# A gated cross-attention block on one core: where TensorE's transposes stand, and the order of an attention step

## The reference, cut to what matters

```python
x = x + tanh(g_xattn) * attention(layernorm(x), ctx, ctx)     # x: (2, 2048, 512), ctx: (2, 77, 512)
x = x + tanh(g_ffn)   * ffn(layernorm(x))

# attention, 16 heads of 32
q, k, v = q_in @ Wq.T, ctx @ Wk.T, ctx @ Wv.T
scores = einsum('bhqd,bhkd->bhqk', q, k) * SCALE
scores = where(row >= key, scores, -1e9)                       # 77 keys: masks the first rows only
out = einsum('bhqk,bhkd->bhqd', softmax(scores), v) @ Wo.T

# ffn, 512 -> 1536 -> 512, integer weights times 1/127
h = silu(x @ wg.T) * (x @ wu.T)
out = h @ wd.T
```

## Time and profile before

| | before |
|---|---|
| median of 3 runs | 873.64 us (873.36 to 874.93) |
| the profiled execution's own time | 874.07 us |
| its span, first to last instruction | 872.3 us |
| PE busy | 98% |
| DVE / ACT / POOL busy | 75% / 53% / 46% |
| mean granted clock of TensorE | 1.000 |

### The profile page before, as it was taken

The page is one execution under the profiler, slowest core; times in us unless marked ns, Lnnn a source line. Parts: engine busy times, 40 slices in busy tenths (PEclk is TensorE's granted clock), DMA queues, the critical chain, the costliest instruction groups (busy, mean ns, idle before and its releaser), DMA issues.

```text
span 872.3 us, 12869 instructions
## 1 busy us (share of the span) xinstructions
PE 855.0 (98%) x4087; PEld 707.9 (81%) x4087; DVE 652.8 (75%) x1081; ACT 460.5 (53%) x1130; POOL 402.3 (46%) x344
## 2 busy tenths in 40 slices
PE   8999999999999999999999999999999999999997
PEld 7678888888888887788888888888888888888876
DVE  5988877778786877679688478788487877587882
ACT  5687575666666757446056264165362364460550
POOL 4665555556564664437144444155253255251350
PEclk9999999999999999999999999999999999999999
DMA  9233847272728131567333256043265143243302
GB/s 334 73 109 118 276 152 248 84 240 93 233 97 277 68 113 51 198 235 265 115 123 133 96 190 249 12 165 121 79 248 182 47 164 113 96 166 116 97 31 98
DMA packets 60406, 128.73 MB, mean 148 GB/s; under 512 B 7616, under 2 KB 20416, under 8 KB 60352
## 3 DMA queue, kind: packets, MB, share of 16 engines
q1 hardware_dynamic: 58960, 125.95, 41.7%
q10 hardware_dynamic: 1392, 2.10, 0.7%
HBM read 99.93 MB, written 27.79 MB: 146 GB/s over the span
## 4 chain that ended last, share of the span: by engine, by line
PE 87%; DVE 6%; ACT 3%; issue 1%; DMA 1%; POOL 1%; ACTq 0%; DVEq 0%
PE psum L1814 34%; PE psum L1548 29%; PE psum L1864 18%; PE psum L1573 4%; DMA gates<-g_ffn 1%; PE psum L1657 1%; ACT e L791 1%; POOL hT L696 1%; DVE bn L1034 1%; DVE e L1076 1%; DVE K L1128 1%; DVE mx L1073 1%; DVE qT L1058 0%; DVE pT L1047 0%; DVE aT L1058 0%
## 5 line engine op out<-in xcount | busy, mean ns | idle before, releaser
L1814 PE MATMUL psum<-xv,ring 128*128 128x512 f32 x1344 | 308.2, 390 | 0.9 <-ACT a L964 0.7
L1814 PEld LDWEIGHTS psum<-xv,ring 128*128 128x128 f32 x1344 | 251.5, 188 | 55.1 <-ACT a L964 1.1
L696 POOL TENSOR_TENSOR hT<-th,hT 128x512 fp32r<-128x512 f32 x48 | 86.3, 1798 | 201.2 <-ACT hT L984 201.2
L1864 PE MATMUL psum<-w_d,hT 128*128 128x512 f32 x768 | 177.7, 391 | 1.3 <-POOL hT L696 0.8
L1864 PEld LDWEIGHTS psum<-w_d,hT 128*128 128x128 f32 x768 | 143.7, 188 | 32.6 <-POOL hT L696 2.0
L554 POOL TENSOR_TENSOR e<-e,rden 128x616 f32<-128x616 f32 x64 | 77.9, 1217 | 110.4 <-DVE rden L1110 73.8
L791 ACT ACTIVATE e<-psum,nmx,q_scale 128x77 f32<-128x77 f32 x256 | 102.6, 427 | 2.3 <-DVE nmx L1090 2.2
L952 ACT ACTIVATE a<-psum 128x512 f32<-128x512 f32 x48 | 28.7, 599 | 131.7 <-PE psum L1814 131.4
L1428 DVE SCALAR_TENSOR_TENSOR acc<-psum,gate_ffn,acc 128x512 f32<-128x512 f32 x64 | 47.7, 750 | 65.1 <-PE psum L1864 65.1
L1548 PE MATMUL psum<-wo,aT 128*128 128x512 f32 x384 | 95.2, 399 | 0.5 <-DVE aT L1058 0.5
L1548 PE MATMUL psum<-xT,wq 128*128 128x512 f32 x360 | 89.0, 398 | 0.4 <-DVE qT L1058 0.4
(11 more groups left out here) (110 smaller groups left out, 1204.6 us busy)
## 6 DMA issues: line engine op xcount, KB each, us to landing
ring<-w_var SPq DMA_DIRECT2D x48, 896.0 KB, 4.6
w_var<-stage SPq DMA_DIRECT2D x12, 896.0 KB, 4.6
x_ln<-x SPq DMA_DIRECT2D x32, 256.0 KB, 4.6
x_res<-x SPq DMA_DIRECT2D x32, 256.0 KB, 5.0
x_mid<-x_res SPq DMA_DIRECT2D x32, 256.0 KB, 2.0
x<-x_mid SPq DMA_DIRECT2D x16, 512.0 KB, 5.6
acc<-x_mid SPq DMA_DIRECT2D x16, 512.0 KB, 6.4
out<-acc SPq DMA_DIRECT2D x32, 256.0 KB, 2.0
```

Source lines behind the costliest of these rows:

```text
L696: nc.gpsimd.tensor_tensor(hT[:, 1, i % HH, j, :], h[:, :], hT[:, 0, i % HH, j, :].bitcast(f32), ALU.subtract).then_inc(h_lo, 1)
L1814: last = nc.tensor.matmul(psum[:, bank, :], stat, mov, start=start and j == 0, stop=j == len(terms) - 1, skip_group_check=not start)
L1864: last = nc.tensor.matmul(m_bank[t % 2][:, :], hT[:, a, m, t // TT, (t % TT) * P:(t % TT + 1) * P], w_d[:, HH * h + m, :], start=m == 0 an ...
```

## The change

Four things are drawn anew.

1. In blocks 1 to 6 the transposes of the probabilities no longer stand in runs. A helper `pieces` hands a product a function that issues one transpose behind each of its matmuls: `o(0, 0, 8, 0)` is the first projection with pieces 0 to 7 of tile 0, one behind each matmul from matmul 0; `o(1, 8, 10, 6)` the second with pieces 8 and 9 behind matmuls 6 and 7.
2. The order of a step: weighted product 0 stands between the two units of tile 0's scores; all transposes of tiles 2 and 3 go inside the query products, and query product 3 ends the step. VectorE's, ScalarE's and GpSimd's lists of a step are written anew to go with it (`last_step`, for block 7, keeps the order that it had).
3. At the end of attention, B22 and B21 go inside weighted products 2 and 3, and VectorE takes the four rests of the weighted products before T2 and T3 are formed.
4. At a pair's end, `p7` stands ahead of `p5` in the last slice, `p4` and `p3` follow at once, and all four groups go inside matmuls of `down`; `down` of tile 1 is cut behind slot 3 and not behind slot 5.

The number of matmuls and transposes stays what it was: 352 transposes (240 of probabilities, 112 of rows) now stand alone.

```diff
+            def pieces(n, t, first, end, at):
+                def after(j):
+                    if at <= j < at + end - first:
+                        turn_piece(n, t, first + j - at)
+                return after
 ...
-            def query(i, m):
+            def query(i, m, after=None):
                 m_wait(i)
                 product(m_bank[m % 2][:, :],
-                        [(wq[:, a, k, m * P:(m + 1) * P], xT[:, c, k, :]) for k in range(KD) for a, c in CROSS]
-                        ).then_inc(m_full, 1)
+                        [(wq[:, a, k, m * P:(m + 1) * P], xT[:, c, k, :]) for k in range(KD) for a, c in CROSS],
+                        after).then_inc(m_full, 1)
 ...
-            def step(n, b, b_before, masked, more):
+            def step(n, b, b_before, masked):
 ...
+                score_unit(n, 0, 0, b, masked, base - 2)
+                v(0)
+                score_unit(n, 0, 1, b, masked, base)
+                v(1)
+                v(2)
+                v(3)
+                scores(n, 1, b, False)
+                pe.wait_ge(m_free, base + 4)
+                pe.wait_ge(wo_split, 2)
+                o(0, 0, 8, 0)
+                o(1, 8, 10, 6)
+                scores(n, 2, b, False)
+                o(2, 0, 8, 0)
+                o(3, 8, 10, 6)
+                scores(n, 3, b, False)
+                pe.wait_ge(x_lo, 4 * n + 8)
+                q(0, 2, 0, 8, 0)
+                q(1, 2, 8, 10, 6)
+                q(2, 3, 0, 4, 6)
+                q(3, 3, 4, 10, 2)
 ...
-            for m in range(G):
-                values(M_LAST + m, m, B - 1, T_P2 - 2 + min(m, 2))
-                if m == 1:
-                    turn(0, B22)
-            turn(0, B21)
+            values(M_LAST, 0, B - 1, T_P2 - 2)
+            values(M_LAST + 1, 1, B - 1, T_P2 - 1)
+            values(M_LAST + 2, 2, B - 1, T_P2, turning(0, B22))
+            values(M_LAST + 3, 3, B - 1, T_P2, turning(0, B21))
 ...
-                    p5(i)
-                    p7(i)
+                    if m == MH - 1:
+                        p7(i)
+                        p5(i)
+                    else:
+                        p5(i)
+                        p7(i)
 ...
-                if more:
-                    turn(p + 1, B11)
-                    turn(p + 1, B12)
                 p4(last)
                 p3(last)
-                down(p, 1, 0, range(HH - 1))
-                down(p, 1, 1, range(HH - 1))
+                if more:
+                    first_k, second_k = turning(p + 1, B11), turning(p + 1, B12)
+                    down(p, 1, 0, range(HH - 1), lambda i: first_k(i) if i < KH * TT else second_k(i - KH * TT))
+                    down(p, 1, 1, range(HH // 2), lambda i: second_k(i + 2 * (HH - 1) - KH * TT))
+                else:
+                    down(p, 1, 0, range(HH - 1))
+                    down(p, 1, 1, range(HH // 2))
 ...
                 down(p, 1, 0, range(HH - 1, HH))
-                down(p, 1, 1, range(HH - 1, HH))
+                down(p, 1, 1, range(HH // 2, HH))
                 if more:
-                    turn(p + 1, B22)
-                    turn(p + 1, B21)
-                for t in range(2, PT):
+                    down(p, 1, 2, range(HH), turning(p + 1, B22))
+                    down(p, 1, 3, range(HH), turning(p + 1, B21))
+                for t in range(4 if more else 2, PT):
                     down(p, 1, t)
```

VectorE's list of a step (`slot(i)` is one tile of statistics: all eight in blocks 1 and 6, `slot` 1, 3, 4 and 5 in the others), up to the shift of tile 1, and the other lists in short:

```diff
+                slot_free(n, 0)
+                shift0(n, 0)
+                v_low(n, 0)
+                largest1(n, 0)
+                offset1(n, 0)
+                slot(0)
+                v_low(n, 1)
+                sum0(n, 0)
+                slot(1)
+                v_low(n, 2)
+                inverse0(n, 0)
+                denominator1(n, 0)
+                slot(2)
+                v_low(n, 3)
+                slot_free(n, 1)
+                shift(n, 1)
 ...
 (GpSimd)
-                probabilities(n, 0)
                 x_low_t(n + 1, (0, 1))
+                probabilities(n, 0)
+                build(n, 0)
                 probabilities(n, 1)
                 x_low_t(n + 1, (2, 3))
                 probabilities(n, 2)
-                if first:
-                    variance(n + 1)
-                build(n, 0, first)
+                build(n, 1)
 ...
 (VectorE, end of attention)
             for m in range(G):
                 m_low(H_LAST + m + 1, m, aT[:, 1, m, :], aT[:, 0, m, :])
-                if m == 1:
-                    form(0, T2)
-                if m == 2:
-                    form(0, T3)
+            form(0, T2)
+            form(0, T3)
+            residual(NB, 0)
             xv_low(0, B21, b21_at)
-            residual(NB, 0)
+            residual(NB, 1)
 ...
 (ScalarE, a pair's end)
-                if more:
-                    xv_copy(p + 1, B11, b11_at)
                 tanh2(last)
                 tanh1(last)
+                h_high(last, 0)
                 if more:
-                    b12_copy(p + 1)
-                h_high(last, 0)
+                    xv_copy(p + 1, B11, b11_at)
                 h_high(last, 1)
```

More of the change, by code:

```diff
@@ L386, in load_w, with residual @@
                     .then_inc(w_in[i % 3], 16)
-            def residual(n, first=False, ahead=False, keeps=((), ())):
+            def residual(n, first=False, ahead=False, keeps=((), (), ())):
                 for t in range(TT):
@@ L400, in residual @@
                     sp.dma_start(mid_f[n - 1, :, t, :], x_res[:, t, :]).then_inc(mid_out[t], 16)
+                    if t == 0:
+                        for more in keeps[1]:
+                            keep(n, 0, more)
                     if ahead and t == 1:
@@ L404, in residual @@
                         load_xs(n + 2)
-                for more in keeps[1]:
+                for more in keeps[2]:
                     keep(n, 0, more)
@@ L628, in build, with first_step, block @@
                     .then_inc(var_built, 1)
-            def block(n, ahead, first=False):
+            def first_step():
+                probabilities(1, 0)
+                x_low_t(2, (0, 1))
+                weigh(1, 1, 0)
+                variance(2)
+                weigh(1, 1, 1)
+                x_low_t(2, (2, 3))
+                probabilities(1, 2)
+                build(1, 0, True)
+                probabilities(1, 3)
+                score_scale(2)
+                variance(3)
+                build(1, 1)
+            def block(n, ahead):
+                x_low_t(n + 1, (0, 1))
                 probabilities(n, 0)
-                x_low_t(n + 1, (0, 1))
+                build(n, 0)
                 probabilities(n, 1)
@@ L865, in first_block, with step, p, weighted @@
                 p(3, 2)
-            def step(n, query):
+            def step(n):
+                def p(t, r):
+                    p_high(n, t, r, 3 * t + r)
+                def weighted(m):
+                    m_high(m_base(n) + m, m, aT[:, 0, m, :])
+                def q(m):
+                    m_high(m_base(n) + 8 + m, m, qT[:, 0, m, :])
+                weighted(0)
+                x_high_t(n + 1, 0)
+                exp0(n, 0)
+                x_high_t(n + 1, 1)
+                weighted(1)
+                exp1(n, 0, lambda: weighted(2))
+                weighted(3)
+                x_high_t(n + 1, 2)
+                x_high_t(n + 1, 3)
+                p(0, 0)
+                exp0(n, 1)
+                p(0, 1)
+                exp1(n, 1)
+                p(0, 2)
+                p(1, 0)
+                exp0(n, 2)
+                p(1, 1)
+                exp1(n, 2)
+                p(1, 2)
+                p(2, 0)
+                exp0(n, 3)
+                p(2, 1)
+                q(0)
+                exp1(n, 3)
+                q(1)
+                p(2, 2)
+                p(3, 0)
+                q(2)
+                p(3, 1)
+                p(3, 2)
+                q(3)
+            def last_step(n):
                 def p(t, r):
@@ L1308, in step @@
                 p(0, 2)
-                st(0)
-                if query:
-                    residual(n, 1)
                 slot_free(n, 2)
@@ L1544, in _, with product @@
         def _(pe):
-            def product(dst, terms):
+            def product(dst, terms, after=None):
                 for j, (stat, mov) in enumerate(terms):
                     last = nc.tensor.matmul(dst, stat, mov, start=(j == 0), stop=(j == len(terms) - 1))
+                    if after is not None:
+                        after(j)
                 return last
@@ L1852, in p3, with down @@
                 strassen(i, set_c[i % 2], S4, B22, p3_full, False)
-            def down(p, h, t, slots=range(HH)):
+            def down(p, h, t, slots=range(HH), after=None):
                 i = M_P2 + 16 * p + PT * h + t
```

281 lines of the change are left out of this document (156 added, 125 removed).

## The result

| | before | after |
|---|---|---|
| median, both on one chip | 873.5 us (873.31 to 874.93) | 879.31 us (879.14 to 879.88, 4 runs) |
| the profiled execution's own time | 874.07 us | 879.18 us |
| its span | 872.3 us | 877.4 us |

The ratio is 1.0065, with an interval of [1.0052, 1.0078]: slower by 0.65%. The forecast was 874.8 with a range of 870.5 to 878.5, so the time lies outside it, on the slow side.

The account below looks back on a forecast made before the run. TensorE, busy 98% at 2.4 GHz, was taken to bound the kernel; 1.9 - 3.2 + 1.7 + 0.2 + 0.9 - 0.3 = +1.2 on 874.07 gave 875.3, or 874.8 us as a median, range 870.5 to 878.5.

Parts of the forecast that it names:

- term e: Pair ends: the wait for GpSimd's rest goes, one ahead of `p4` comes; together -0.3 us, between -1 and +1.
- the wait at `hT`: Pair ends: PE's wait for GpSimd's rest, 0.42 us start to start and 0.1 for the load, goes three times.
- a, transposes alone: 352 transposes standing alone cost 0.119 us each, 41.9 against 40.0 now: +1.9 us, ends -0.9 and +6.8.
- Rival 1: A transpose alone costs its columns only, 0.054 us; about 854 us in all; chance 0.08.
- The reason that I gave: The next matmul's weights load from the transpose's start and take about its pitch, so the load is late either way.
- b, waits that go: Small PE waits inside the six steps of blocks 1 to 6, 3.8 us in all; 3.2 us taken back.
- c, new waits: Projection 0 waits for the rest of weighted product 3, mostly in blocks 1 and 6: +1.7 us, between 0 and 4.
- The wait for late rows of block 3: In block 1 the fifth slot's rows land about 1.5 us after VectorE asks, costing 0.3 us.
- Rival 3: Projection 0 waits in every step behind ScalarE's exponentials; 878 us in the middle, 880 at worst; chance 0.23.
- Block 7: Its second score unit waits 0.7 us, before about 0.1; a wait in its weighted products goes: +0.2 us.
- d, end of attention: Transposes now end before weighted product 3 does, so 1.58 us ahead of the projections stand empty: +0.9 us.

Follow-up runs that it names:

- `price`: The kernel before with patterns of matmuls and transposes on TensorE alone added at its very end; a matmul with a transpose measured 0.347 us.
- the second part: The kernel before with further TensorE patterns at its end, M's rows halved too; matmuls of 64 and 128 rows in turn measured 0.853 us for two.

## Why the prediction was wrong

**The step that failed is term e**, the pair ends: "Together -0.3, between -1 and +1". Measured are +1.59, +1.61 and +1.53 in the three pairs and -0.5 in the last stretch, +4.2. I followed `p7`, `p4` and `p3`, and that part came much as written: 0.25 + 0.11 of waiting ahead of `p4` where I had 0.45 and no load behind it, the wait at `hT` gone. But moving the transposes of B22 and B21 into matmuls made them end 4.8 us later, and I didn't follow what waits for them. VectorE's list has results 3 and 4 behind the pieces that come out of those transposes, and `down` of tiles 5 and 6 wants the banks that these results free. The working named no wait behind `p3` but the old one at `hT`. The two waits for these results cost 1.30 us a pair, 3.9 in all, and the experiment that moved only the two results gave 4.0 back. With it the time is 875.33, 0.5 from the forecast. That this is so near is in part luck: in the steps the forecast was 0.9 too low, and block 7 (0.2) and the head (0.5) lay the other way.

**The rest, term by term**, against the forecast's +1.2 of sum (measured +5.1 in the spans):

- a, transposes alone: 0.119 predicted, 0.118 measured. In the steps 1.0 predicted, 1.10 measured. Rival 1 (columns only, 854) is out. The reason that I gave stood the test only in the end: halving the columns spoke against it, and matmuls in place of transposes and the rows of loads bore it out. What no run bears out in it is that a load goes by its columns.
- b, waits that go: 3.2 predicted. The steps give 252.20 + 1.10 + 1.7 - 252.62 = 2.4, with term a and the new waits as measured. That is the low end I had worked out, 2.5, from the shortest step; I took the middle. The shortest step, block 6's, had no masked products and no idle time on PE, though VectorE did more in it than in blocks 3 to 5 (34.12 us against 32.1), so it was the better measure of a step without waits.
- c, new waits: 1.7 predicted, 0.64 + 0.52 + 3 x 0.15 + 0.08 = 1.7 measured. The place, blocks 1 and 6, and the cause, a tile of statistics ahead of the rest, were right, and the slot's move took it away. The wait for late rows of block 3 did not come: nothing of it shows in block 1's stretch. Rival 3 (projection 0 late by half a microsecond in every step) is out too.
- Block 7: +0.2 predicted, -0.03 measured. Its new wait is there (0.72 + 0.105, predicted 0.7 + 0.1), but what went inside the stretch was as large. The wait in its weighted products I had taken at its idle 0.33; from start to start it cost 0.49 + 0.08.
- d, end of attention: +0.9 predicted, +0.97 measured, and given back whole.
- The head, which I didn't price, was 0.5 shorter in this execution; between the kernels here it varies by nearly as much with nothing changed there (first step at 60.59 in `price` and 60.91 in before, at 60.43 to 60.87 in the variants of after).

**Rivals.** The terms ask which wait takes the place of the one removed at projection 0, in block 7, at the end of attention and ahead of `p4`; among the rivals only projection 0 got a price of its own. The same mechanism decided at 490 us and in the next two pair ends, where the question was not asked.

## What to carry to other kernels

When a group of instructions is spread out, its last one ends later, and everything that waits for it moves too. List these on each engine, and then what stands *behind* them in the same in-order list, above all whatever frees a bank. A 128x128 transpose is no cheaper here between long matmuls than in a run, 0.12 us against 0.11, so spreading transposes gains nothing by itself. What gained was the order of a step, with its transposes put back into runs: 1.6 us once the results, the statistics and the end of attention were left in their places.

## What the hardware showed beyond that

- The floor of a matmul with its own weights is 0.112 us, for 64 as for 128 columns; with 256 columns beside a matmul of 512 it costs 0.122. Only a run of transposes with 64 rows and 64 columns went faster, 0.064. Why it does, when alone it costs 0.120, stays open, and so does what bounds the load, if it isn't the columns.
- Two row counts in turn cost 0.20 us at each change (0.426 against 0.227 a matmul). The rows of weights show idle time ahead of every load there. Two column counts of the weights in turn, 64 and 128, cost nothing of the kind (0.342 and 0.340 for M and T, against 0.347). The Trainium skill, "TensorEngine Tiling (Array Packing)", section "Key Properties", says that a change of the tiling mode drains TensorE. The 0.20 fits that if 64 and 128 rows are two modes; the columns' 64 and 128 don't show it.
- With 128 rows and then 64 rows at 64 columns in turn, PE was "busy" all the time by the page, and still the granted clock fell from 2.4 to 1.2 GHz in the middle of it (0.99, then 0.50 in the windows above). A pair took 0.63 us before it fell and 1.02 after. In the pattern of the second part, with 64 and 128 rows but 512 columns in both, it stayed at the upper level.
- A wait that PE meets ahead of a matmul costs its length and some 0.11 us more, 0.10 to 0.115 in nearly all of them (0.08 in one of before's), since the weights behind the first are not loaded ahead.
